# Half of the mixed adapter rows moved into the idle rows of the down projection's third tile, with the tail of TensorE's order rewritten

## The reference

```python
out = x @ W.T                                   # W: 512 x 352
a = jnp.einsum('th,krh->tkr', x, qa)            # 8 adapters of rank 8: 64 values a token
b = jnp.einsum('tkr,khr->tkh', a, qb)
mix = jnp.einsum('tkh,tk->th', b, w)            # w: the token's weights of the 8 adapters
return out + scale[None, :] * mix
```

## Time and profile before

| | |
|---|---|
| median of the runs | 1694.26 us |
| fastest and slowest run | 1688.27, 1695.64 us |
| span of the profiled execution, first to last instruction | 1685.8 us |
| TensorE (matmul) | 1568.4 us busy, 93% |
| VectorE | 1155.5 us, 69% |
| GpSimd | 737.8 us, 44% |
| ScalarE | 617.2 us, 37% |
| mean granted TensorE clock | 0.977 |

### The profile page before, as it was taken

The page is one execution under the profiler, slowest core; times in us unless marked ns, Lnnn a source line. Parts: engine busy times, 40 slices in busy tenths (PEclk is TensorE's granted clock), DMA queues, the critical chain, the costliest instruction groups (busy, mean ns, idle before and its releaser), DMA issues.

```text
span 1685.8 us, 19547 instructions
## 1 busy us (share of the span) xinstructions
PE 1568.4 (93%) x6856; PEld 1155.1 (69%) x6856; DVE 1155.5 (69%) x1634; ACT 617.2 (37%) x971; POOL 737.8 (44%) x537
## 2 busy tenths in 40 slices
PE   3787799798888999999999999999999999999999
PEld 2343377566666677777777777777777777777776
DVE  5798964788999867487888755778888553333333
ACT  5545443444454434443343244333433321111111
POOL 4488510489898801077777301376786000000000
PEclk8799999899999999999999999999999999999999
DMA  7688627688787664765667445587665456566552
GB/s 251 215 285 315 254 80 253 201 290 297 270 289 286 253 255 172 248 228 205 232 238 258 152 161 196 202 275 257 238 208 180 175 200 210 184 222 222 195 181 85
DMA packets 111473, 375.87 MB, mean 223 GB/s; under 512 B 20176, under 2 KB 45776, under 8 KB 94864
## 3 DMA queue, kind: packets, MB, share of 16 engines
q1 hardware_dynamic: 101904, 340.81, 57.8%
q10 hardware_dynamic: 9472, 33.82, 5.8%
HBM read 304.33 MB, written 70.25 MB: 222 GB/s over the span
## 4 chain that ended last, share of the span: by engine, by line
PE 63%; DVE 18%; issue 5%; ACT 5%; POOL 4%; DMA 3%; SPq 0%; ACTq 0%; DVEq 0%; POOLq 0%
PE b_g L735 14%; PE b_u L735 14%; PE b_u L826 7%; DVE ring L1493 4%; PE b_g L826 3%; PE b_q L781 3%; PE b_q L826 3%; PE b_g L799 2%; DVE ring L1499 2%; PE b_g L766 2%; DVE tt L1467 2%; POOL ring L1392 2%; PE b_g L759 1%; POOL yx L1401 1%; DVE z L1467 1%
## 5 line engine op out<-in xcount | busy, mean ns | idle before, releaser
L1392 POOL TENSOR_TENSOR ring<-du,rep 128x512 f32<-128x512 f32 x256 | 344.5, 1349 | 151.4 <-DVE du L1571 91.9
L735 PE MATMUL b_g<-xnb,gm 128*128 128x512 f32 (+1 forms) x1440 | 356.2, 396 | 0.9 <-DVE xnb L1470 0.9
L735 PE MATMUL b_u<-xnb,gm 128*128 128x512 f32 (+1 forms) x1440 | 349.1, 391 | 0.0
L1493 DVE TENSOR_TENSOR_SCAN ring<-b_a,ring 128x512 f32<-128x512 f32 x256 | 310.8, 1214 | 15.7 <-ACT b_a L964 8.4
L1401 POOL TENSOR_TENSOR yx<-yx,ring 128x512 f32<-128x512 f32 x192 | 261.8, 1364 | 130.4 <-DVE ring L1499 129.9
L735 PEld LDWEIGHTS b_g<-xnb,gm 128*128 128x128 f32 (+1 forms) x1440 | 252.1, 179 | 89.1 <-issue 24.6
L735 PEld LDWEIGHTS b_u<-xnb,gm 128*128 128x128 f32 (+1 forms) x1440 | 257.1, 179 | 71.1
L1467 DVE SCALAR_TENSOR_TENSOR tt<-tt,b_g 128x512 f32<-128x512 f32 (+1 forms) x120 | 82.1, 684 | 222.7 <-ACT tt L964 222.5
L964 ACT ACTIVATE b_a<-delta,a_neg 128x512 f32<-128x512 f32 x256 | 173.6, 681 | 113.9 <-DVE ring L1493 113.9
L964 ACT ACTIVATE tt<-b_g 128x512 f32<-128x512 f32 (+1 forms) x120 | 71.1, 593 | 316.7 <-PE b_u L766 286.3
L826 PE MATMUL b_u<-dwt,hhl 128*128 128x512 f32 (+1 forms) x720 | 185.4, 394 | 0.0
(11 more groups left out here) (254 smaller groups left out, 2120.2 us busy)
## 6 DMA issues: line engine op xcount, KB each, us to landing
gm<-scr_gm SPq DMA_DIRECT2D x64, 1024.0 KB, 6.8
dwt<-scr_dw SPq DMA_DIRECT2D x32, 1536.0 KB, 6.8
rep<-bc_d ACTq DMA_DIRECT2D x64, 512.0 KB, 5.8
gm<-scr_gm SPq DMA_DIRECT2D x32, 768.0 KB, 4.4
dqt<-scr_dq SPq DMA_DIRECT2D x25, 896.0 KB, 9.1
scr_gm<-gm SPq DMA_DIRECT2D x20, 1024.0 KB, 7.5
scr_dw<-dwt SPq DMA_DIRECT2D x10, 1536.0 KB, 6.2
qat<-scr_qa SPq DMA_DIRECT2D x25, 512.0 KB, 10.2
```

The lines of the kernel that those rows point to most:

```text
L735: i = mm(out_b[0:IW[m], :], w, v, start=(n == 0), stop=(n == 11 and not is_routed(s)))
L1392: v.tensor_tensor(ring[:, T % NRING], du[:, T % 4, :], rep[:, N % NREP, 0], ALU.mult).then_inc(pool_dbu, 1)
L1493: v.tensor_tensor_scan(w, ba[T % 2][:], w, 0.0, ALU.mult, ALU.add).then_inc(dve_scan, 1)
```

## The change

1. `dqt` loses the low part of its last 512 columns. Those columns now hold, by rows: 0 to 31 the high part of qb's first 32 rows, 32 to 63 the low part of the same 32 rows, 64 to 95 the high part again. `daw_s` holds in the same rows the high part, the high part again, and the low part of the first 32 mixed values. One product with 96 rows replaces two with 128.
2. The other 32 mixed values go into rows 96 to 127 of `hh` and `hl`, tile 2, and the other 32 rows of qb into rows 96 to 127 of `dwt`, third tile. The third tile's products of routed experts take 128 rows.
3. On TensorE the products of tile 2 move behind the adapter values, next to `adapter_b`; the next expert's first gate product (`up(s + 1, 0, 0)`) moves ahead of them.
4. ScalarE rounds three times instead of once in `daw_round`; VectorE subtracts twice (32 rows each) instead of one `stt` on 128 rows in `daw_low`; VectorE's `lo_piece` is two instructions for dw (was one) and three for dq (was one); ScalarE's `hi` is two for each.
5. Stores of dw and dq are two DMAs each; dq becomes 640 KB instead of 896 KB. A new tile `hold_x` takes over a use of the end of `dqt`. In the first batch's scan VectorE gets two subtractions (`q3_lo_0`), GpSimd's two for dq become one.

```diff
@@ down, adapter_b, routed (TensorE)
-                    if tc == 0:
+                    if tc == 0 and not (m == IC - 1 and is_routed(s)):
                         pe.wait_ge(dve_hl, IC * s + m + 1)
                     n = 3 * m
-                    k = slice(0, IW[m])
+                    k = slice(0, P if is_routed(s) else IW[m])
...
-                if tc == DONE[0]:
-                    pe.wait_ge(dve_daw, rho(s) + 1)
-                q = slice(IC * P, IC * P + H)
-                mm(down_bank(s, tc)[:], daw_s[:, t], dqt[:, 0, q], start=False, stop=False)
-                mm(down_bank(s, tc)[:], daw_s[:, t], dqt[:, 1, q], start=False, stop=True
-                   ).then_inc(pe_dn, 1)
+                mm(down_bank(s, tc)[:], daw_s[HID, t], dqt[HID, QA:Q_D], start=False, stop=True).then_inc(pe_dn, 1)
...
-                up_waits(s, 0)
-                up(s, 0, 0)
+                if e == 0:
+                    up_waits(s, 0)
+                    up(s, 0, 0)
                 up(s, 0, 1)
...
-                down(s, 0, (2,))
-                down(s, 1, (2,))
-                down(s, 2)
+                down(s, 2, (0, 1))
+                down(s, 3, (0, 1))
                 if post:
                     xn_transposed(b + 1, (2, 3))
-                down(s, 3)
+                if e < NF - 1:
+                    up_waits(s + 1, 0)
+                    up(s + 1, 0, 0)
+                pe.wait_ge(dve_daw, rho(s) + 1)
+                pe.wait_ge(act_daw, 3 * (rho(s) + 1))
                 for tc in DONE:
+                    down(s, tc, (2,))
                     adapter_b(s, tc)
@@ daw_round (ScalarE)
                 act.wait_ge(dve_dawf, rho(s) + 1)
-                rounded(rnd[:], dawf[:]).then_inc(act_daw, 1)
+                rounded(daw_s[:], dawf[:]).then_inc(act_daw, 1)
+                rounded(hh[C1, 2], dawf[C1]).then_inc(act_daw, 1)
+                act.wait_ge(act_daw, 3 * rho(s) + 1)
+                rounded(daw_s[C0B], dawf[C0]).then_inc(act_daw, 1)
@@ lo_piece, daw_low (VectorE)
+                if kind == "dw":
+                    lo(dwt[:, 1, 0:2 * H], src[:, 0:2 * H], dwt[:, 0, 0:2 * H])
+                    lo(dwt[HID, 1, W2], src[HID, W2], dwt[HID, 0, W2]).then_inc(done, 1)
+                    return
+                if kind == "dq":
+                    lo(dqt[:, Q_D:Q_ALL], src[:, 0:QA], dqt[:, 0:QA])
+                    lo(dqt[C0B, QA:Q_D], src[C0, QA:Q_D], dqt[C0, QA:Q_D])
+                    lo(dwt[C1, 1, W2], src[C1, QA:Q_D], dqt[C1, QA:Q_D]).then_inc(done, 1)
+                    return
...
-                dve.wait_ge(act_daw, rho(s) + 1)
-                stt(daw_s[:], rnd[:].bitcast(F32), mlo[:], dawf[:], ALU.mult, ALU.add).then_inc(dve_daw, 1)
+                r = rho(s)
+                dve.wait_ge(act_daw, 3 * r + 1)
+                lo(daw_s[C0C], dawf[C0C], daw_s[C0C])
+                dve.wait_ge(act_daw, 3 * r + 2)
+                lo(hl[C1, 2], dawf[C1], hh[C1, 2]).then_inc(dve_daw, 1)
+
+            def q3_lo_0(n):
+                src = raw_0[n][2]
+                dve.wait_ge(act_s0, n + 1)
+                lo(dqt[C0B, QA:Q_D], src[C0, QA:Q_D], dqt[C0, QA:Q_D])
+                lo(dwt[C1, 1, W2], src[C1, QA:Q_D], dqt[C1, QA:Q_D]).then_inc(dve_q3, 1)
```

More of the change, by code:

```diff
@@ L71, in gated_ssm_moe @@
         PW = [2 * HC * IW[m] for m in range(IC)]
-        Q_D = IC * P + H
+        QA = IC * P
+        Q_D = QA + H
+        Q_ALL = Q_D + QA
+        W2 = slice(2 * H, 3 * H)
+        C0, C0B, C0C, C1 = (slice(k * 32, (k + 1) * 32) for k in range(4))
+        HID = slice(0, IW[2])
         gm = [sb("gm%d" % m, [P, 2, PW[m]], F32R) for m in range(IC)]
-        dwt, dqt = sb("dwt", [P, 2, RAW], F32R), sb("dqt", [P, 2, Q_D], F32R)
+        dwt, dqt = sb("dwt", [P, 2, RAW], F32R), sb("dqt", [P, Q_ALL], F32R)
         qat, qbt = sb("qat", [P, 2, HC * P], F32R), sb("qbt", [P, 2, I], F32R)
@@ L87, in gated_ssm_moe @@
         sb("pr_rest", [P, 2 * PRE_ALL - 2 * RAW])
-        scr = {k: dram("scr_" + k, [NX if k[0] == "g" or k == "dw" else NF, P, 2 * width[k]]) for k in tile_of}
+        scr = {k: dram("scr_" + k, [NX if k[0] == "g" or k == "dw" else NF, P, Q_ALL if k == "dq" else 2 * width[k]])
+               for k in tile_of}
         scr_pr = dram("scr_pr", [P, 2 * PRE_ALL])
@@ L149, in gated_ssm_moe @@
         ctx_raw = ring[:, 0:2]
-        hold = [dqt[:].rearrange("p a n -> p (a n)")[:, m * L:(m + 1) * L] for m in range(HC - 1)]
-        hold.append(qbt[:].rearrange("p a n -> p (a n)")[:, 0:L])
+        hold = [dqt[:, 0:L], dqt[:, L:2 * L], qbt[:].rearrange("p a n -> p (a n)")[:, 0:L], hold_x[:]]
         ctx_h, ctx_l = hold[0:2], hold[2:4]
@@ L408, in load @@
                 free(sp, kind, s)
-                sp.wait_ge(dma_st[kind], 16 * stored_before(kind, s))
+                sp.wait_ge(dma_st[kind], stored(kind) * stored_before(kind, s))
+                if kind == "dw" and s >= NX:
+                    sp.wait_ge(dma_st["dq"], stored("dq") * NF)
+                if kind == "dq":
+                    sp.dma_start(dqt[:].bitcast(F32), scr[kind][w_index(s)]).then_inc(dma_t[kind], 16)
+                    return
                 sp.dma_start(tile_of[kind][:].bitcast(F32).rearrange("p a n -> p (a n)"), scr[kind][w_index(s)]
@@ L797, in adapter_a @@
                 n = 3 * m
-                for w, v in three(dqt[k, 0, o:o + P], dqt[k, 1, o:o + P], hh[k, m], hl[k, m]):
+                for w, v in three(dqt[k, o:o + P], dqt[k, Q_D + o:Q_D + o + P], hh[k, m], hl[k, m]):
                     i = mm(b_g0[:], w, v, start=(n == 0), stop=(n == 8))
@@ L974, in hi @@
                 free(act, kind, s)
-                need(act, dma_st[kind], 16 * stored_before(kind, s))
-                rounded(tile_of[kind][:, 0], raw[slot_of[k]][:, 0:width[kind]]).then_inc(act_hi[slot_of[k]], 1)
+                need(act, dma_st[kind], stored(kind) * stored_before(kind, s))
+                src = raw[slot_of[k]]
+                if kind == "dw":
+                    rounded(dwt[:, 0, 0:2 * H], src[:, 0:2 * H])
+                    rounded(dwt[HID, 0, W2], src[HID, W2]).then_inc(act_hi[slot_of[k]], 1)
+                    return
+                if kind == "dq":
+                    rounded(dqt[:, 0:Q_D], src[:, 0:Q_D])
+                    rounded(dwt[C1, 0, W2], src[C1, QA:Q_D]).then_inc(act_hi[slot_of[k]], 1)
+                    return
+                rounded(tile_of[kind][:, 0], src[:, 0:width[kind]]).then_inc(act_hi[slot_of[k]], 1)
             def hi_0(n):
@@ L983, in hi_0 @@
                 if n >= 4 and (kind[0] == "g" or kind == "dw"):
-                    act.wait_ge(dma_st[kind], 16 if s == 2 else 32)
+                    act.wait_ge(dma_st[kind], stored(kind) * (1 if s == 2 else 2))
+                if kind == "dq":
+                    act.wait_ge(dma_st["dw"], stored("dw"))
+                    rounded(dqt[:, 0:Q_D], src[:, 0:Q_D])
+                    rounded(dwt[C1, 0, W2], src[C1, QA:Q_D]).then_inc(act_s0, 1)
+                    return
+                if kind == "dw" and s == 2:
+                    rounded(dwt[:, 0, 0:2 * H], src[:, 0:2 * H])
+                    rounded(dwt[HID, 0, W2], src[HID, W2]).then_inc(act_s0, 1)
+                    return
                 rounded(tile_of[kind][:, 0], src[:, 0:width[kind]]).then_inc(act_s0, 1)
@@ L1353, in lo_0 @@
                     pool.wait_ge(act_s0, n + 1)
-                i = lo(t[:, 1, o], src[:, o], t[:, 0, o])
+                if kind == "dq":
+                    i = lo(dqt[:, Q_D:Q_ALL], src[:, 0:QA], dqt[:, 0:QA])
+                elif kind == "dw" and raw_0[n][1] == 2 and part == 2:
+                    i = lo(dwt[HID, 1, W2], src[HID, W2], dwt[HID, 0, W2])
+                else:
+                    i = lo(t[:, 1, o], src[:, o], t[:, 0, o])
                 if part == parts_0(n) - 1:
```

31 lines of the change are left out of this document (29 added, 2 removed).

## The result

| | before | changed |
|---|---|---|
| median of the runs on the same chip | 1693.73 us | 1710.67 us (1709.94 to 1714.84, four runs) |
| ratio to before | 1 | 1.0117, interval 1.0094 to 1.0140 |
| span of the profiled execution | 1685.8 us | 1709.0 us |

The change makes the kernel 1.2% slower. The forecast was 1696 us, no change; the time lies above the range of 1680 to 1707.

The account below looks back on a forecast made before the run. TensorE bounds batches 1 to 3, VectorE batch 0's stretch from 366 to 577. Terms -21.8 + 6.3 + 16 + 1.2 = +1.7 us on span 1685.8; median 8.5 above, so 1696 us; own range 1687 to 1702, wider range 1680 to 1707.

Parts of the forecast that it names:

- the 1.2 for the first scan: First batch's scan: VectorE gets two subtractions, GpSimd loses one piece; costs 1.2 us, between 0 and 3.5.
- dq's splits: VectorE, batch 0 bodies: two added subtractions, one paying for a GpSimd turn; 1.8 us an expert (0.7 undisturbed, 2.9 if both).
- the shorter first part of dq: VectorE, batch 0 bodies: dq's first split has 512 columns fewer, saving about 0.5 us.
- Experts 1 and 7 of batch 0: Batch 0: losses of experts 0 and 1 left at nothing; the last expert's saved products worth 0 to 0.9 us.
- The tail in batch 0: VectorE, batch 0 tails: one added subtraction costs 0.6 to 1.75 us an expert, taken as 1.5.
- dw, ScalarE and the order in batch 0: Batch 0, per expert: dw's added subtraction 0.1 us, ScalarE's second dw instruction 0.1; 0.3 back from GpSimd holding up later ones less.
- The new waits in batches 1 and 2: TensorE waits for mixed values in experts 0, 3 and 4: 0.65, 1.25, 1.25 us; 6.3 in all, low end 0.8.
- The products: TensorE, batches 1 to 3: four adapter_b products fewer save 0.91 us an expert, 21.8 over 24; 128-row products cost nothing extra.
- The slower rival: Batch 0: every added subtraction lets one GpSimd instruction through, 24 us over five experts; kernel at 1706 us, chance 0.17.

Follow-up runs that it names:

- x3_q_out: Changed kernel without the two added subtractions behind dqt in batch 0's bodies (left out, so low halves are missing); 1692.31 us, ratio to before 1.0017.
- x7_both: Changed kernel with one subtraction in the tail instead of two, and without the two added behind dqt (left out); 1674.24 us, ratio to before 0.9911.
- x4_order_only: Kernel before with only TensorE's new order of products, keeping the two adapter_b products; 1696.29 us, ratio to before 1.0031.
- x12_x_load_last: New scheme in later batches only, with the next batch's x load queued behind its step's weight loads; 1671.17 us, ratio to before 0.9875.
- x2_q_psum: Changed kernel; batch 0's two added subtractions behind dqt read one operand from PSUM, experts 1 to 6; 1700.78 us, ratio to before 1.0062.
- x8_q_earlier: Changed kernel with dq's three subtractions of batch 0's bodies moved ahead of the scan step, nothing left out; 1698.68 us, ratio to before 1.0055.
- x5_later_batches: Kernel before with the new scheme only in batches 1 to 3 and batch 0's expert 0, one tail subtraction; 1674.20 us, ratio to before 0.9913.

## Why the prediction was wrong, step by step

The working from expert 0's point on, which leaves the scattered setup out: forecast +0.5 (without the 1.2 for the first scan), measured 30.0 - 2.3 - 1.9 - 7.0 = +18.8. The difference of 18.3 is made of these steps.

- **dq's splits: mis-sized, 1.8 us an expert foreseen, 3.4 measured.** This is the step that failed. From the start of dqt's first split to the end of qat's, VectorE's timelines have 3.27, 2.75, 3.60, 3.09 and 4.03 us in experts 2 to 6 before, and 7.50, 4.61, 7.52, 6.60 and 7.50 in the changed kernel: 3.4 more on average. x3_q_out agrees: over these experts the changed kernel loses 22.6 us and x3_q_out, without the two added subtractions, 5.8; the difference is 3.36 each. The step said that one of the two would pay, "because in rows 9 GpSimd had two instructions ready and one was paid for before". Rows 9 are of expert 3, and for expert 3 the step came out, 1.86 us more: both added ones pay, and qat, which paid before, no longer does. Expert 3 is the only one whose VectorE does the row statistics just ahead; in that time GpSimd gets its gm piece done (445.27 to 447.67 in the changed kernel), and two instructions are left to it. VectorE (the first row joins dqt's two, 0.55 and 1.64 us), then GpSimd:

```profile
452.07 2.21 DVE L1531 TENSOR_TENSOR dqt<-raw,dqt 128x384 fp32r<-128x384 f32 x2
454.30 1.66 DVE L1531 TENSOR_TENSOR dwt<-raw,dqt 32x512 fp32r<-32x512 f32 x1
455.99 0.69 DVE L1531 TENSOR_TENSOR qat<-raw,qat 128x512 fp32r<-128x512 f32 x1
```

```profile
452.24 1.50 POOL L1462 TENSOR_TENSOR yx<-yx,ring 128x512 f32<-128x512 f32 x1 [2.14 <-DVE ring L1570]
453.82 1.59 POOL L1453 TENSOR_TENSOR ring<-du,rep 128x512 f32<-128x512 f32 x1
```

In the other four experts the gm piece of 2.4 us stands ahead, and the splits cost 3.5 to 4.2 more. The trace of the kernel before shows that too: in expert 4, where dqt's split starts at 475.42, GpSimd runs four instructions without a wait between them.

```profile
473.96 2.41 POOL L1337 TENSOR_TENSOR gm<-raw,gm 128x1024 fp32r<-128x1024 f32 x1 [2.39 <-ACT gm L964]
476.33 2.14 POOL L1401 TENSOR_TENSOR yx<-yx,ring 128x512 f32<-128x512 f32 x1
478.55 1.61 POOL L1392 TENSOR_TENSOR ring<-du,rep 128x512 f32<-128x512 f32 x1
480.12 1.54 POOL L1401 TENSOR_TENSOR yx<-yx,ring 128x512 f32<-128x512 f32 x1
```

One expert was read as typical of five. Nor did the shorter first part of dq save its 0.5: it went from 1.70 to 2.05 on average.

- **Experts 1 and 7 of batch 0: at nothing, 7.3 us measured** (4.0 and 3.4). Without the added subtractions of body and tail together (x7_both) they lose 0.0. The sum gives no reason: "What experts 0 and 1 lose I leave at nothing", and of the last expert it weighs only the saved products (0 to 0.9 us), while what grows there is VectorE's work. In expert 1 the splits from dqt to qat take 5.93 us instead of 3.89. In expert 7 nothing holds them up; counted from expert 6's point, VectorE is 2.3 us later behind that expert's tail and 1.0 more behind the longer list of splits.
- **The tail in batch 0: right.** 1.5 foreseen; x3_q_out less x7_both over experts 2 to 6 is 7.4 us, 1.48 each.
- **dw, ScalarE and the order in batch 0: small, as foreseen.** About -0.1 foreseen, or -0.6 with the shorter first part of dq, which x7_both keeps; x7_both has -1.6 over five experts, -0.3 each.
- **The new waits in batches 1 and 2: 6.3 foreseen, 9.7 measured** (16 x 0.87 less the 4.2 that came back). The subtraction's part was right in kind and near in size: one subtraction instead of two gives 7.4. What was not seen at all is the queue: the new order holds dwt longer (its load is issued 10.5 us behind batch 1's point of expert 0 in x4_order_only, 7.8 in the kernel before), all loads behind it start later, and qat comes late. x4_order_only shows it without the change's other parts, and x12_x_load_last takes it away.
- **The products: right.** 0.87 against 0.91 an expert; over 24 experts 20.9 instead of 21.8. The 128-row products cost nothing extra, and batch 3 gave 7.0.

The parts are 6.6 (batch 0, experts 2 to 6: 22.6 against 16), 7.3, 3.4 and 0.9, together 18.2. The slower rival named the mechanism, "every added subtraction in batch 0 lets one GpSimd instruction through", and gave 4.8 us an expert; 4.5 were measured. Its argument against, "at most two instructions ready", fell with the same reading of one expert.

What it rests on is shown from two sides: dq's added subtraction costs 0.68 instead of 1.63 us with an operand in PSUM (x2_q_psum), and as little where GpSimd is idle (x8_q_earlier, and expert 7 of the changed kernel). The page "SBUF — State Buffer" of the Trainium skill, section "Who interferes with whom", has both conditions: a VectorE instruction with at most one SBUF input, outside the two-port modes, does not contend with GpSimd, and one with two SBUF inputs does, with a GpSimd instruction that reads SBUF, the one issued second blocking until the first is done. The traces agree (0.68 beside a running GpSimd instruction in x2_q_psum, 1.63 behind one in the changed kernel). The prediction quoted that rule and then discounted it.

Open: what of the changed kernel's 5.6 us at expert 0 is its own, since that point scatters by 13 us from one profiled execution to the next; and what of x5_later_batches' 3.7 us in batch 0 comes from its longer list of stores: x12_x_load_last, with the same stores, loses 1.2, so a good part may be scatter.

## What to carry to other kernels

Where VectorE and GpSimd share a stretch, count VectorE's instructions with two SBUF operands, not their size: each can cost a whole GpSimd instruction, so one subtraction on 64 rows is far cheaper than two on 32, and rearranging rows is better left to a DMA that is stored anyway. Before a cost per iteration is set, look at every iteration: the one with extra work ahead of the place is the one in which the other engine has caught up. When an order frees a buffer later, follow the queue that waits for it up to the last load behind it.
